# The attention's value products in four column tiles instead of two, with row sums prepared on GpSimd

## The reference

```
def _L0_attn_ref(x, Wq, Wk, Wv, Wo):
    B, S, H = (16, 128, 512)
    NH, NKV = (16, 4)
    HD = H // NH
    ...
    b, s, _ = x.shape                      # 2, 1024 by the inputs
    ...
    k = jnp.repeat(k, rep, axis=1)
    v = jnp.repeat(v, rep, axis=1)
    scores = jnp.einsum('bhqd,bhkd->bhqk', q, k) * scaling
    attn = jax.nn.softmax(scores, axis=-1)
    out = jnp.einsum('bhqk,bhkd->bhqd', attn, v)
```

## Time and profile before

| | |
|---|---|
| median of 3 runs (lowest, highest) | 1762.67 us (1762.53, 1763.45) |
| profiled execution: its own time | 1759.44 us |
| its span, first to last instruction | 1757.6 us |
| mean granted TensorE clock | 0.982 |
| PE busy | 1670.2 us, 95% |
| DVE, ACT, POOL busy | 843.1, 659.2, 550.9 us |

### The profile page before, as it was taken

One profiled execution on the slowest core, in us unless ns is written; L12 is line 12 of the kernel. 1 busy time (PEld: TensorE's weight loads), 2 busy tenths in 40 slices (PEclk: granted clock), 3 DMA queues, 4 the chain that ended last, 5 costly groups with the idle time before them and its releaser, 6 DMA issues.

```text
span 1757.6 us, 23172 instructions
## 1 busy us (share of the span) xinstructions
PE 1670.2 (95%) x8164; PEld 1180.3 (67%) x8164; DVE 843.1 (48%) x1522; ACT 659.2 (38%) x974; POOL 550.9 (31%) x574
## 2 busy tenths in 40 slices
PE   6998999999998989999999999999999999999997
PEld 5676898998876753444444444434877889999985
DVE  5553322222477766666666666622655432222226
ACT  4422222222233245555455555564442222323220
POOL 3115476316559520000000000010131527641745
PEclk9998999999998989999999999999999999999998
DMA  9215444334462211100001000003010535433427
GB/s 347 94 46 203 160 175 169 131 106 146 132 195 72 69 40 28 25 19 19 19 22 34 19 19 19 1 25 124 33 45 31 212 141 183 174 135 105 151 82 244
DMA packets 67835, 175.62 MB, mean 100 GB/s; under 512 B 10769, under 2 KB 11665, under 8 KB 65425
## 3 DMA queue, kind: packets, MB, share of 16 engines
q1 hardware_dynamic: 54896, 100.48, 17.6%
q0 software_dynamic: 12832, 73.67, 11.9%
HBM read 102.29 MB, written 55.84 MB: 90 GB/s over the span
## 4 chain that ended last, share of the span: by engine, by line
PE 77%; DMA 8%; DVE 6%; ACT 3%; issue 3%; POOL 2%; SPq 0%; DVEq 0%; POOLq 0%; ACTq 0%
PE PS L1332 14%; PE PS L1086 9%; PE PS L1088 9%; PE PS L1087 9%; PE PS L1300 9%; PE PS L1319 7%; DMA xn<-x_routed 5%; DMA xs<-x_routed 2%; PE PS L1223 2%; PE PS L1228 2%; PE PS L1226 2%; PE PS L1225 2%; PE PS L1227 2%; PE PS L1224 2%; PE PS L1191 2%
## 5 line engine op out<-in xcount | busy, mean ns | idle before, releaser
L1563 ACT ACTIVATE PT<-PS 128x1024 f32<-128x1024 f32 x256 | 261.8, 1023 | 220.4 <-PE PS L1319 219.1
L1332 PE MATMUL PS<-PT,V 128*33 128x512 f32 x1024 | 259.2, 607 | 0.0
L1861 DVE TENSOR_REDUCE nmf_later<-PS 128x1 f32<-128x1024 f32 x160 | 195.6, 1223 | 130.6 <-PE PS L1300 130.6
L1920 POOL TENSOR_TENSOR W<-raw,W 128x544 fp32r<-128x544 f32 x144 | 190.0, 1351 | 1.5
L1300 PE MATMUL PS<-KS,QS 96*128 96x512 f32 x512 | 185.7, 445 | 3.6 <-DVE nmf_first L1861 1.6
L1300 PEld LDWEIGHTS PS<-KS,QS 96*128 96x128 f32 x512 | 79.1, 192 | 147.4 <-issue 95.6
L1319 PE MATMUL PS<-QS,KS 98*128 98x512 f32 x512 | 174.6, 422 | 2.7 <-DVE nmf_later L1861 1.3
L2015 POOL CAST Wo<-woraw 128x512 fp32r<-128x512 f32 x4 | 2.6, 644 | 540.7 <-DMA woraw<-wo 540.7
L1828 DVE TENSOR_TENSOR thid<-thid,PS 128x352 f32<-128x352 f32 x78 | 40.6, 521 | 245.7 <-ACT thid L1501 245.7
L1086 PE MATMUL PS<-xh,W 128*128 128x512 f32 x352 | 141.4, 402 | 4.8 <-DVE xl L1588 1.6
L1861 DVE TENSOR_REDUCE nmf_first<-PS 128x1 f32<-128x1024 f32 x96 | 116.2, 1221 | 53.7 <-PE PS L1300 53.5
(11 more groups left out here) (187 smaller groups left out, 3372.9 us busy)
## 6 DMA issues: line engine op xcount, KB each, us to landing
raw<-ffn_w POOLq DMA_DIRECT2D x18, 2176.0 KB, 10.3
y_routed<-ytile SPq DMA_DIRECT2D x78, 256.0 KB, 2.1
xn<-x_routed SPq DMA_DIRECT2D x40, 256.0 KB, 3.2
x_routed<-xq SPq DMA_DIRECT2D x1, 9984.0 KB, 29.5
xs<-x_routed SPq DMA_DIRECT2D x38, 256.0 KB, 3.3
QS<-later_hi SPq DMA_DIRECT2D x112, 64.0 KB, 2.0
raw<-ffn_w SPq DMA_DIRECT2D x6, 768.0 KB, 9.9
raw<-ffn_w SPq DMA_DIRECT2D x16, 272.0 KB
```

The lines of the kernel that those rows point to most:

```text
L1332: mm = e.matmul(PS[j * COLS:j * COLS + VCOL, ob, :], V[:, b * QT + 2 * pair + j, g, :], PT[:, u % PTBUF, j * GRP:(j + 1) * GRP], start=pai ...
L1563: e.activation(PT[:, u % PTBUF, :], PS[:, i:i + 2, :].rearrange("p b n -> p (b n)"), ACT.Exp, scale=SCALE).then_inc(p_ready.sem, 1)
L1861: e.tensor_reduce(row_maxima(n)[:, h, t:t + 1], PS[:, i:i + 2, :].rearrange("p b n -> p (b n)"), AX.X, ALU.max, negate=True).then_inc(max_ ...
L1920: low = e.tensor_tensor(W[:, slot, 1, cs], raw[slot][:, cs], W[:, slot, 0, cs], ALU.subtract)
```

## The change

A half-head's 8 key tiles are now multiplied in three rounds of three, three and two (`ROUNDS`). Each key tile takes a quarter of TensorE's columns (`QUARTER`, 32); `V` loses its column of ones. The fourth quarter multiplies a single column of ones (`one_col`) and puts its result on partition 96. In round 0 it takes key tile 0, in round 1 key tile 1, and in round 2 `added`: the sum of key tiles 2 to 7. That sum is made by three additions in `add_up`: units 1 and 2 (128x1024), plus unit 3 (128x1024), then the two halves of the result (128x512). GpSimd does it, except for the second half of each head in the last group, where VectorE does.

The rounds stand beside units 0, 1 and 2 of the next half-head, and the store of a half-head beside unit 0 of the one after. `PT` has 8 buffers instead of 4 and lies where X was. `turn_queries` and `place_queries` move from units 8 and 9 of 16 to units 5 and 6. The DVE reduction behind the transposes adds three parts of 32 instead of two of 33.

```diff
+PTBUF = 8
+ROUNDS = ((0, 1, 2), (3, 4, 5), (6, 7))
+QUARTER = P // 4
+SUMS_ROW = 3 * QUARTER
...
-        due = {2: [], 3: [u - LAG - 1, u - LAG]}.get(pair, [u - LAG])
-        for w in due if u >= LAG else ():
-            work.append(("values", w))
-        if outputs and pair == 2:
-            work.append(("store_head", *outputs.pop(0)))
-        outputs.extend(unit(w)[:3] for w in due if u >= LAG and ends_half(w))
+        hh = u // (QT // 2) - 1
+        if hh >= 0 and pair == 0:
+            work.extend([("sum", hh), ("values", hh, 0)])
         if n + 1 < groups:
             work.append(("row_max", n + 1, un // QT, un % QT))
+        if outputs and pair == 0:
+            work.append(("store_head", *outputs.pop(0)))
+        if hh >= 0 and pair in (1, 2):
+            work.append(("values", hh, pair))
+            if pair == 2:
+                outputs.append(half_head(hh))
...
-        if n + 2 < groups and un % (UNITS // 2) == 8:
+        if n + 2 < groups and un % (UNITS // 2) == 5:
             work.append(("turn_queries", n + 2, un // (UNITS // 2)))
-        if n + 2 < groups and un % (UNITS // 2) == 9:
+        if n + 2 < groups and un % (UNITS // 2) == 6:
             work.append(("place_queries", n + 2, un // (UNITS // 2)))
...
+    def add_up(e, lane, done, hh):
+
+        u, to = hh * (QT // 2), added[:, hh % 2, :]
+        lane.wait_ge(p_ready, u + 2)
+        if hh >= 2:
+            lane.wait_ge(pv_done, hh - 2, 2)
+        e.tensor_tensor(to, PT[:, (u + 1) % PTBUF, :], PT[:, (u + 2) % PTBUF, :], ALU.add).then_inc(done.sem, 1)
+        lane.wait_ge(done, hh, 0)
+        lane.wait_ge(p_ready, u + 3)
+        e.tensor_tensor(to, to, PT[:, (u + 3) % PTBUF, :], ALU.add).then_inc(done.sem, 1)
+        lane.wait_ge(done, hh, 1)
+        e.tensor_tensor(to[:, 0:GRP], to[:, 0:GRP], to[:, GRP:], ALU.add).then_inc(done.sem, 1)
...
-            for j in range(2):
-                mm = e.matmul(PS[j * COLS:j * COLS + VCOL, ob, :], V[:, b * QT + 2 * pair + j, g, :],
-                              PT[:, u % PTBUF, j * GRP:(j + 1) * GRP], start=pair == 0, stop=ends_half(u))
-            mm.then_inc(pv_done.sem, 1)
+            for i, kt in enumerate(ROUNDS[round_]):
+                u = hh * (QT // 2) + kt // 2
+                pe.wait_ge(p_ready, u)
+                e.matmul(PS[i * QUARTER:(i + 1) * QUARTER, ob, :], V[:, b * QT + kt, g, :],
+                         PT[:, u % PTBUF, kt % 2 * GRP:(kt % 2 + 1) * GRP],
+                         start=round_ == 0, stop=kt + 3 >= QT)
+            if round_ < 2:
+
+                src = PT[:, hh * (QT // 2) % PTBUF, round_ * GRP:(round_ + 1) * GRP]
+            else:
+                pe.wait_ge(added_dve if sums_on_vector(hh) else added_pool, hh, 2)
+                src = added[:, hh % 2, 0:GRP]
+            e.matmul(PS[SUMS_ROW:SUMS_ROW + 1, ob, :], one_col[:], src,
+                     start=round_ == 0, stop=round_ == 2).then_inc(pv_done.sem, 1)
```

More of the change, by code:

```diff
@@ L187, in unit, with half_head, sums_on_vector @@
     return n, un // QT, un // (QT // 2) % 2, un % (QT // 2)
-def ends_half(u):
-    return u % (QT // 2) == QT // 2 - 1
+def half_head(hh):
+    return unit(hh * (QT // 2))[:3]
+def sums_on_vector(hh):
+    n, _, hf = half_head(hh)
+    return n == len(KV_GROUPS) - 1 and hf == 1
 def beside_heads(n):
@@ L446, in order_of_work @@
     end = groups * UNITS
-    for w in range(end - LAG, end):
-        work.append(("values", w))
-    work.append(("store_head", *unit(end - 1)[:3]))
+    hh = end // (QT // 2) - 1
+    work.extend([("sum", hh), ("values", hh, 0), ("store_head", *outputs.pop(0)), ("values", hh, 1), ("values", hh, 2),
+                 ("store_head", *half_head(hh))])
     work.append(("attention_end",))
@@ L574, in macaron @@
     OT, behind = place("OT", (P, GRP), F32, at)
-    nmf_first, _ = place("nmf_first", (P, REP, QT), F32, behind)
+    nmf_first, behind = place("nmf_first", (P, REP, QT), F32, behind)
+    one_col, _ = place("one_col", (P, 1), F32, behind)
     ropeS, _ = place("ropeS", (P, QT, 2, HD), F32, at)
@@ L590, in macaron @@
     QS = [place(f"QS{i}", (P, REP, S), F32R, g_at[FIRST[i]])[0] for i in range(3)]
-    PT, at = place("PT", (P, PTBUF, 2 * GRP), F32, g_at[LATE])
+    PT, at = place("PT", (P, PTBUF, 2 * GRP), F32, x_at)
+    assert at <= x_at + NT * D * 4
+    added, at = place("added", (P, 2, 2 * GRP), F32, g_at[LATE])
     assert at <= g_at[LATE] + group_bytes
     assert ORDER[0] * TPG // QT == 1
-    Wo, at = place("Wo", (P, 2, DC, D), F32R, wqkv_at - NT // 2 * NKV * VCOL * 4)
+    Wo, at = place("Wo", (P, 2, DC, D), F32R, wqkv_at - NT // 2 * NKV * HD * 4)
     woraw, _ = place("woraw", (P, D), F32, arena + NT * D * 4 + NKV * S * 4)
@@ L599, in macaron @@
     rL, at = place("rL", (P, 2, TPG), F32, at)
-    head, at = place("head", (P, 2, TPG, VCOL), F32, at)
+    head, at = place("head", (P, 2, TPG, HD), F32, at)
     nmf_later, at = place("nmf_later", (P, 2 * REP, QT), F32, at)
@@ L833, in macaron @@
         elif kind == "values":
-            u = key[0]
-            pv_done.plan(u)
-            if ends_half(u):
-                ot_ready.plan(*unit(u)[:3])
+            hh, round_ = key
+            pv_done.plan(hh, round_)
+            if round_ == 2:
+                ot_ready.plan(*half_head(hh))
+        elif kind == "sum":
+            hh, = key
+            for i in range(3):
+                (added_dve if sums_on_vector(hh) else added_pool).plan(hh, i)
         elif kind == "store_head":
@@ L932, in macaron @@
     head_place = {key: i for i, key in enumerate(heads)}
-    ends = [tuple(unit(key[0])[:3]) for kind, *key in work
-            if kind == "values" and ends_half(key[0])]
+    ends = [tuple(half_head(key[0])) for kind, *key in work if kind == "values" and key[1] == 2]
     end_place = {key: i for i, key in enumerate(ends)}
@@ L941, in heads_over @@
     def heads_over(lane):
[L943 removed]
+        lane.wait_ge(pv_done, last_half, 2)
         lane.wait_ge(ot_turned, *heads[-1])
@@ L1787, in store_head @@
             q = head_place[n, h, hf] % 2
-            o = PS[:, MISC, :].rearrange("p (j a c) -> p j c a", j=TPG, c=COLS)[:, :, 0:VCOL, :]
+            o = PS[:, MISC, :].rearrange("p (j a c) -> p j c a", j=TPG, c=QUARTER)
             dve.wait_ge(ot_turned, n, h, hf)
-            e.tensor_reduce(head[:, q, :, :], o, AX.X, ALU.add).then_inc(halves_summed.sem, 1)
+            dve.step(e.reciprocal(rL[:, q, :], o[:, :, 0, 3]))
+            e.tensor_reduce(head[:, q, :, :], o[:, :, :, 0:3], AX.X, ALU.add).then_inc(halves_summed.sem, 1)
+            dve.after_step()
             dve.wait_ge(halves_summed, n, h, hf)
-            dve.step(e.reciprocal(rL[:, q, :], head[:, q, :, HD]))
-            dve.after_step()
             t0, c0 = b * QT + hf * TPG, (g * REP + h) * HD
@@ L1872, in vector_program @@
                     dve.wait_ge(home_out[g])
+            elif kind == "sum" and sums_on_vector(*key):
+                add_up(e, dve, added_dve, *key)
             elif kind == "store_head":
@@ L2011, in gpsimd_program @@
                 pool.wait_ge(max_turned, 0, REP - 1)
+            elif kind == "sum" and not sums_on_vector(*key):
+                add_up(e, pool, added_pool, *key)
             elif kind == "wo":
```

46 lines of the change are left out of this document (22 added, 24 removed).

## The result

The changed kernel takes 1677.47 us, the median of 4 runs (1674.46 to 1678.58). The kernel before takes 1763.06 on the same chip (1762.53 to 1766.01). The ratio is 0.9509 with a 95% interval of 0.9492 to 0.9525, so the change gains 85.6 us. I had forecast 61, and my range ended at 1688. The direction is right, and so is the price of a round; the size is not: about 25 us came from terms that I had costed at nothing or too low.

The account below looks back on a forecast made before the run. TensorE, busy 95% of the span, was taken to bound the kernel; 49 + 18 + 1.6 - 6 - 0.5 - 1 = 61 us gained, giving 1702 us (0.66, own range 1690 to 1715); overall range 1688 to 1748.

Parts of the forecast that it names:

- The round: Value products on PE: a round of tiles side by side takes 1.01 us.
- rival 1: Value rounds: TensorE streams only two different operands at a time, a round takes 1.84 us; 1854 us, slower; chance 0.10.
- rival 2: Value rounds: each of two further tiles adds an unhidden weight load of 0.11 us, round 1.20; 1734 us; chance 0.11.
- The turned queries: PE's twelve waits for `later_lo` before a result's transposes go whole: 18 us.
- The chain: GpSimd's three additions, 6.3 us, hidden in main groups; in the last group 1.6 us lost four times, 6 us.
- The last group's half-head: Half-heads without row maxima: 5.9 us after the change, 7.5 where POOL adds.
- The scaling: A head's scaling on DVE, held up by GpSimd's additions: 0.8 us mean, not 0.3, nothing counted.
- rival 3: DVE's scaling, locked by GpSimd's additions, delays row maxima; PE waits 0.9 us in 56 half-heads; 1752 us; chance 0.11.
- small pieces: Main half-heads: the step sum gives 8.6 for 8.88 us now, less 0.1 of transpose of maxima and small waits.
- The rounds: Value products of 64 half-heads: 3.80 us falls to 3.03, 0.77 us each, 49 us gained.
- The wait on `OT`: Ahead of the last group's transposes: 0.2 us in each of 8 half-heads goes, 1.6 us.
- The late start of the values: First half-head: values come two units later, none computed beside it, so DVE's row maxima pace it: 1 us lost.

Follow-up runs that it names:

- experiment 1: The kernel before, with its queries turned and split one unit earlier (units 7 and 8 of each 16); 1730.46 us, ratio 0.9888 to the kernel before.
- experiment 4: The changed kernel without its additions, the last round multiplying constant ones, so the sums of rows are not computed; 1655.09 us, ratio 0.9464 to before.
- experiment 3: The changed kernel's order, `PT` buffers and turned queries' place, but the products of before: two tiles of 33 columns, no GpSimd additions; 1708.88 us, ratio 0.9766.
- experiment 2: The changed kernel with rounds 1 and 2 ahead of the row maxima of their unit instead of behind them; 1697.71 us, ratio 0.9698 to before.
- experiment 5: The changed kernel measured again, nothing altered; 1674.78 us, ratio 0.9502 to before.
- experiment 6: The changed kernel with all 8 additions of the last group on VectorE; 1670.46 us, ratio 0.9470 to before.
- experiment 9: The kernel before with queries turned one unit earlier and values in four equal stretches per half-head instead of three; 1743.52 us, ratio 0.9875 to before.

## Why the prediction came out 25 us short

**What held.** The round: 1.01 forecast, 0.99 measured, and rival 1 (1.84) and rival 2 (1.20) are out. The turned queries: 18 forecast, 17.2 measured in experiment 1. GpSimd: 2.43 for 1024 columns forecast, 2.44 and 2.39 measured, 1.28 for 512 (forecast 1.30). The chain is hidden in the main groups; in the last it costs 1.76 us at a time (forecast 1.6), 6.9 in all (forecast 6), and 0.84 at the end (forecast 0.5). The last group's half-head, 5.9 forecast, is 5.73. That its half-heads with GpSimd's sum take 7.49 us, as the prediction said (7.5), is luck in part: the half-head was 0.17 too long and the wait 0.16 too short. The scaling at 0.90 us mean (forecast 0.8), with no wait of PE from it: rival 3 is out by experiment 4.

**The step that failed.** In the paragraph on GpSimd's additions I wrote of the half-head: "8.6 by the same sum stands for 8.88 now, less 0.1 of such pieces". The sum of free-running steps fell 0.3 us short of the measured half-head, I put it down to small pieces that stay, but for 0.1, and "The sum" has no term for them, not even for that 0.1. They were not small pieces that stay. Nearly all of it was the wait for the row maxima: scores 0.17 late once in each half-head, and 0.12 of weight loads that came late with them. In the new order a round stands between every row maximum and the scores that take its banks, and both are gone. That is 16 us in the main groups (experiment 3), and experiment 2 shows it from the other side. The rows were there: from the row maximum at 778.92 to the values at 780.32 it is 1.40 us, where the same products from 775.49 to 776.62 took 1.13, and I gave those 0.27 us no term. My question, what takes the place of a removed wait, I asked of DVE's room and never of the scores.

**Terms that were mis-sized.** The rounds: 49 forecast, 53 measured, 0.84 a half-head instead of 0.77. I took 3.80 - 3.03; by the steps it is 3.81 - 2.96 (0.989 + 0.989 + 0.982) = 0.85. The start of more weight loads costs 0.006 us a round, not 0.025, and the round with three tiles nothing (0.982, where the prediction also had a figure of 1.08). The wait on `OT` in the last group: 0.30 a half-head, not 0.2. The clock behind the waits for `later_lo`: 4.8 us, not forecast. The late start of the values: 1 us forecast. From the first scores to the first store it takes 15.8 us before and 18.3 after (18.1 to 20.3 in the experiments with this order, 16.8 with the table loaded ahead), so 2.3 to 4.5 us without that, of which a part comes back behind the last scores; the ledger has it in the order's net.

**The ledger,** from the first scores to the last store, by intervals of store to store:

| | us | forecast |
|---|---|---|
| four tiles at once (experiment 3 to 4) | 53 | 49 |
| wait for `later_lo` (experiment 1) | 17 | 18 |
| clock falls behind it (experiment 1) | 5 | 0 |
| order: row maxima and loads 16, OT, change of groups, end, later start, net (experiment 1 to 3) | 18 | 1.6 - 1 |
| additions: waits 6.9, end 0.8, a clock fall 1.6 (experiment 4) | -9 | -6.5 |
| start of the attention, not the same in all runs (experiment 4) | 2 | 0 |
| sum | 86 | 61 |

Measured 85.6. Experiments 1 and 3 are 19.7 us apart in this stretch; 1.6 of them are the fall of the clock in experiment 1 that the row on the order leaves out. The range was too narrow on this side because its lower end came from the bare cost of a round alone (0.98), and held nothing for an order that changed around every unit.

## What to carry to other kernels

Add up the free-running steps of the period that repeats and compare the sum with the measured period: every tenth of a microsecond that is left is a wait to be named before the change is priced, since an edit that reorders work may take it away or double it. Look for it in the steps from start to start, not in PE's wait rows: a late start of 0.17 us stood in none of them here, and showed, if at all, in those of the weight loads. And a burst of products belongs between the maxima that keep a bank busy and the scores that want it: that place was worth about 16 us here, and 33 were lost when two of the three rounds were moved away from it.

## What the runs showed of the chip that I had not expected

- Four column tiles, each with its own moving data of 512 float32 columns, take 0.989 us where two take 0.983: no sign of a limit at two streams (round 1 of the changed kernel).
- TensorE's clock fell to 1.2 GHz behind 3 of 12 waits of 1.5 us that were followed by transposes, and stayed up behind the other 9; behind the wait of 1.3 us at the change of groups it fell in two traces (the changed kernel's first, experiment 1) and stayed up in four (before, experiments 3, 5 and 6). What decides was not found.
- A product that starts late cost more than its idle time: 0.17 us of wait came with 0.12 us more in the steps into the value products, which I read as weight loads that came late.
- A further stretch of value products cost 0.28 us by the steps of experiment 9, of which only 0.12 lies in the stretch; the rest is in the steps ahead of it and behind it.
- A lock between DVE and GpSimd that triples an instruction (0.29 to 0.90 us) was free in the main groups: PE's half-heads are the same with it and without it.
